# Semaphores set by SyncE ahead of a stage, one table load, and an in-place Newton step in a fused perceiver layer

## The reference

```python
B, S, dim, SKV, cdim, H, D = 16, 64, 256, 1601, 128, 16, 128
q = rmsnorm(layernorm(x) @ Wq, gq)               # per head, over D
k = rmsnorm(ctx @ Wk, gk);  v = ctx @ Wv         # per head
x = x + softmax(q @ k.T / sqrt(D)) @ v @ Wo
q, k, v = layernorm(x) @ W_qkv, each quantised by its own largest magnitude
x = x + softmax(q8 @ k8.T * scales / sqrt(hd)) @ v8 * v_scale @ W_out + b_out
x = x + causal attention with one key head and value head a token, chosen by argmax(softmax(x @ W_gate.T))
```

## Time and profile before

| what | us |
|---|---|
| median of 3 runs (lowest to highest) | 1481.54 (1479.16 to 1481.94) |
| the profiled execution's own time | 1480.01 |
| its span | 1478.0 |
| TensorE busy in it | 1386.3 (94%) |
| TensorE's weight loads | 936.6 (63%) |
| VectorE busy | 1259.4 (85%) |
| ScalarE busy | 1202.5 (81%) |
| GpSimd busy | 982.6 (66%) |
| query stage | 0 to 139.5 |
| key loop | 142.5 to 1237 |
| end of the loop | 1237 to 1318 |
| last stage | 1318 to 1478 |

### The profile page before, as it was taken

The page is one execution under the profiler, slowest core; times in us unless marked ns, Lnnn a source line. Parts: engine busy times, 40 slices in busy tenths (PEclk is TensorE's granted clock), DMA queues, the critical chain, the costliest instruction groups (busy, mean ns, idle before and its releaser), DMA issues. The chain is left out here.

```text
span 1478.0 us, 31543 instructions
## 1 busy us (share of the span) xinstructions
PE 1386.3 (94%) x5980; PEld 936.6 (63%) x5980; DVE 1259.4 (85%) x5006; ACT 1202.5 (81%) x4843; POOL 982.6 (66%) x1505
## 2 busy tenths in 40 slices
PE   5997999999999999999999999999999999966886
PEld 4664666666666666666666666666666666854554
DVE  6776888998989898889989898998998998756985
ACT  5886889898898989898988988898989887535763
POOL 4000788888989898889889898988888885010000
PEclk9998999999999999999999999999999999986998
DMA  4000000000000000000000000000000001000000
GB/s 143 38 1 1 1 2 24 4 21 16 10 23 1 24 1 23 2 23 2 23 13 13 23 1 25 1 23 2 23 1 27 22 30 64 1 1 1 8 7 16
DMA packets 9849, 25.30 MB, mean 17 GB/s; under 512 B 736, under 2 KB 6016, under 8 KB 9520
## 3 DMA queue, kind: packets, MB, share of 16 engines
q1 hardware_dynamic: 9648, 23.49, 4.4%
HBM read 22.44 MB, written 1.05 MB: 16 GB/s over the span
## 5 line engine op out<-in xcount | busy, mean ns | idle before, releaser
L1014 ACT ACTIVATE c_unused<-c_prod 124x128 f32<-124x128 f32 x1664 | 493.1, 298 | 83.6 <-DVE c_prod L1238 77.5
L1554 POOL TENSOR_TENSOR c_acc<-c_acc,c_prob 123x1024 f32<-123x1024 f32 (+1 forms) x192 | 461.9, 2406 | 23.9 <-ACT c_prob L1021 23.2
L1249 DVE CUSTOM_DVE_ANT_0 c_multiplied<-psK,c_c 124x128 f32<-124x128 f32 x1664 | 381.5, 285 | 57.0 <-PE psK L809 57.0
L808 PE MATMUL psK<-wkh,c_cTh 128*124 128x512 f32 x832 | 413.5, 497 | 10.9 <-DVE c_cTl L1277 9.2
L828 PE MATMUL psO<-c_prob,raw 123*128 123x512 f32 (+1 forms) x832 | 392.1, 594 | 0.0
L1238 DVE TENSOR_TENSOR c_prod<-psK,c_c 124x512 f32<-124x512 f32 x416 | 286.0, 688 | 53.4 <-PE psK L809 40.1
L809 PE MATMUL psK<-wkl,c_cTh 128*124 128x512 f32 x832 | 329.6, 396 | 0.0
L1014 ACT ACTIVATION_READ_ACCUMULATOR c_unused<-c_prod 124x1 f32 x1664 | 311.3, 187 | 0.0
L1260 DVE TENSOR_TENSOR c_prob<-psS,c_ss 124x512 f32<-124x512 f32 x416 | 265.7, 680 | 0.5 <-POOL c_ss L1537 0.5
L1021 ACT ACTIVATE c_prob<-c_prob,shift 124x1024 f32<-124x1024 f32 x208 | 236.6, 1137 | 0.4 <-DVE c_prob L1260 0.4
L808 PEld LDWEIGHTS psK<-wkh,c_cTh 128*124 128x124 f32 x832 | 154.2, 185 | 114.7 <-DVE c_ss L1249 47.5
(11 more groups left out here) (314 smaller groups left out, 2165.2 us busy)
## 6 DMA issues: line engine op xcount, KB each, us to landing
raw<-in_ctx SPq DMA_DIRECT2D x16, 799.5 KB
raw<-in_L_xattn_Wq SPq DMA_DIRECT2D x3, 512.0 KB, 9.5
xs<-in_x SPq DMA_DIRECT2D x1, 1024.0 KB, 5.8
big<-in_L_xattn_Wk SPq DMA_DIRECT2D x1, 1024.0 KB, 8.7
c_prod<-in_L_xattn_Wo SPq DMA_DIRECT2D x1, 1024.0 KB, 5.3
out<-s_y SPq DMA_DIRECT2D x8, 128.0 KB, 1.7
big<-in_L_ffn_W_qkv SPq DMA_DIRECT2D x1, 768.0 KB, 12.5
raw<-in_L_xattn_Wv SPq DMA_DIRECT2D x1, 768.0 KB, 4.1
```

What stands on the lines that cost most here:

```text
L808: nc.tensor.matmul(psK[0:ROWS, c % 2, :], cTh[:, slot, :], T.wkh[:, cols], start=True, stop=False)
L1014: last = nc.scalar.activation(unused[:, j, :], prod[:, k % 2, c // 2, j * CD:(j + 1) * CD], ACT.Copy, accum_out=ss[:, k % 2, 0, h:h + 1])
L1249: last = nc.vector.tensor_tensor_reduce(multiplied[:, j, :], psK[0:ROWS, 1, cols], c2[:, k % NT, :], 1.0, 0.0, ALU.mult, ALU.add, ss[:, k ...
L1554: nc.gpsimd.tensor_tensor(acc[0:rows, batch % 2, :], acc[0:rows, batch % 2, :], prob[0:rows, probs(s), :], ALU.add).then_inc(S.acc, 1)
```

## The change

1. `primed` is split into `signals` (makes the semaphores) and `set_signals` (sets them). The semaphores of the second and third stage are made ahead; SyncE sets those of the second while the first stage runs, behind its loads, and those of the third (68 of them) at the head of its block in the second. No block for either. Only the first stage keeps `primed`.
2. The table of functions is loaded in the first stage only.
3. Query stage: x comes in four DMAs and Wq in halves; statistics and normalisation go by halves of x; the sum of squares becomes two fp32r matmuls with GpSimd making the high part (an addition of a broadcast 0 that rounds to fp32r) and the low part; it moves one item later, beside the logarithm, and waits for `root` of two items before; the logarithm stands first on ScalarE. `scaled` goes and its value is written over the sum in PSUM. All of Wk's transposes and splits, and the splits of Wq's second to fourth quads, move into the first steps; GpSimd makes the low parts of Wq in pieces of 256 columns at the first twelve items, and clears `raw` in four pieces at items 20 to 23. The gain's maximum moves from items 28 and 30 to 25 and 28.
4. Key loop: `newton_start` writes its result over the bank, `newton_end` reads it there, and TensorE's wait at line 837 (and in `turn`) is for `dfull` instead of `dneg`.
5. `end`: `matrices(1)` and `segment(0)` before the denominators, `segment(1)` before `turn(2)`, with the other engines' order to match.
6. Last stage: five semaphores become two, `found` and `swept`.

```diff
@@ -133,10 +133,23 @@
+def signals(nc, ctx, plain, *loops):
+
+    zero, made = semaphores(nc, ctx, *plain), [semaphores(nc, ctx, *group) for group in loops]
+    return (zero, *made), [(sem, 0) for sem in zero] + [(sem, CREDIT) for group in made for sem in group]
+
+
+def set_signals(eng, sems):
+
+    for sem, value in sems:
+        eng.sem_clear(sem)
+        if value:
+            eng.sem_inc(sem, value)
...
@@ queries, SyncE
             sp.dma_start(wqkv, dram["L0_ffn_W_qkv"].rearrange("(k p) n -> p k n", p=P)).then_inc(S.wqkv, 16)
             sp.dma_start(wgate, dram["L0_ffn_W_gate"]).then_inc(S.wgate, 16)
-            sp.wait_ge(S.zeroed, 1)
+            set_signals(sp, T.later)
+            sp.wait_ge(S.zeroed, len(ZERO))
...
@@ queries, GpSimd, step(n, m, o)
+                pool.wait_ge(S.square, m + 1)
+                if m >= 2:
+                    pool.wait_ge(S.total, m - 1)
+                nc.gpsimd.tensor_tensor(squareh[:, m % 2, :], square[:, m % 2, :], blank[:, :].broadcast_to([P, BANK]), ALU.add).then_inc(S.squareh, 1)
+                pool.wait_ge(S.squareh, m + 1)
+                nc.gpsimd.tensor_tensor(squarel[:, m % 2, :], square[:, m % 2, :], squareh[:, m % 2, :].bitcast(F32), ALU.subtract).then_inc(S.squarel, 1)
...
@@ queries, TensorE
-                if m is not None:
-                    pe.wait_ge(S.square, m + 1)
-                    if m >= 2:
-                        pe.wait_ge(S.newton, m - 1)
-                    nc.tensor.matmul(psS[:, m % 2, :], T.ones[:, :], square[:, m % 2, :], start=True, stop=True).then_inc(S.total, 1)
...
+                    pe.wait_ge(S.squarel, o + 1)
+                    if o >= 2:
+                        pe.wait_ge(S.root, o - 1)
+                    nc.tensor.matmul(psS[:, o % 2, :], onesr[:, :], squareh[:, o % 2, :], start=True, stop=False)
+                    nc.tensor.matmul(psS[:, o % 2, :], onesr[:, :], squarel[:, o % 2, :], start=False, stop=True).then_inc(S.total, 1)
...
@@ cross_attention, TensorE, denominators
                 if den_bank(i, batch, half) is psM_all:
-                    pe.wait_ge(S.dneg, batch_done(i, batch, 2, half))
+                    pe.wait_ge(S.dfull, batch_done(i, batch, 2, half))
@@ cross_attention, TensorE, end
             def end(i, batch):
-                denominators(i, batch, 0)
-                pe.wait_ge(W.vTl, 2)
-                denominators(i, batch, 1)
                 matrices(1)
                 segment(0)
+                denominators(i, batch, 0)
+                denominators(i, batch, 1)
+                segment(1)
                 turn(2)
                 turn(3)
-                segment(1)
@@ cross_attention and self_attentions, ScalarE
-            nc.scalar.preload_act_table_set(LN_EXP)
@@ cross_attention, VectorE
             def newton_start(i, batch, half):
                 dve.wait_ge(S.dinv, batch_done(i, batch, 2, half + 1))
-                nc.vector.scalar_tensor_tensor(den[:, 2, :], den_bank(i, batch, half), -1.0, den[:, 1, :], ALU.mult, ALU.mult).then_inc(S.dneg, 1)
+                nc.vector.scalar_tensor_tensor(den_bank(i, batch, half), den_bank(i, batch, half), -1.0, den[:, 1, :], ALU.mult, ALU.mult).then_inc(S.dneg, 1)
             def newton_end(i, batch, half):
                 dve.wait_ge(S.dneg, batch_done(i, batch, 2, half + 1))
                 dve.wait_ge(S.norm, batch_done(i, batch, 2, half))
-                nc.vector.scalar_tensor_tensor(den[:, 3, :], den[:, 2, :], 2.0, den[:, 1, :], ALU.add, ALU.mult).then_inc(S.dfull, 1)
+                nc.vector.scalar_tensor_tensor(den[:, 3, :], den_bank(i, batch, half), 2.0, den[:, 1, :], ALU.add, ALU.mult).then_inc(S.dfull, 1)
```

More of the change, by code:

```diff
@@ L181, in load_context @@
     sp.dma_start(raw[FULL:ROWS, b, 0:REST, :], one[:, FULL * NT:SKV, :]).then_inc(sems[1], 16)
-PREP_SEMS = ("x gains wk wq0 wq1 wq2 wq3 consts gprod made stats moments centred lnT lnTh lnTl wkT wkTh wkTl wqh wql "
-             "gram gramh graml zeroed context m8 m2 sel causal iota selb wgate wqkv turn turned gT gtop gall")
+PREP_SEMS = ("x0 x1 x2 x3 gains wk wq0 wq1 wq2 wq3 consts gprod made stats moments centred lnT lnTh lnTl wkT wkTh wkTl wqh wql "
+             "wql0 onesr blank gram gramh graml zeroed context m8 m2 sel causal iota selb wgate wqkv turn turned gT gtop gall")
 Q_SLOTS = 3
 X_SLOTS = 2 * BANK // DIM
-ITEM_SEMS = "q square qgh qgl total log y half newton root qw out"
+ITEM_SEMS = "q square squareh squarel qgh qgl total log y half newton root qw out"
 def queries(nc, T, psum, dram):
@@ L252, in queries, with low_part @@
         gain_row, gain_all = psM[0:1, 0:P], psM[:, P:P + 1]
-        GAIN_AT, GAIN_ALL_AT = 28, 30
+        GAIN_AT, GAIN_ALL_AT = 25, 28
+        WK_AT, WQ_AT = ((0, 1), (2, 3)), (0, 1, 3)
+        wk_banks = (psO[:, 0, :], psO[:, 1, :], psT[:, :], psM[:, :])
+        FIRST = (NPAIR // 2) // PW
+        def low_part(m):
+            q, k, part = 1 + m // 4, m // 2 % WC, m % 2
+            return (q, k, part) if q < KC else None
+        ZERO_AT = (20, 21, 22, 23)
+        ZERO = [slice(2 * NT * CD * n // 4, 2 * NT * CD * (n + 1) // 4) for n in range(4)]
         def out(n):
@@ L337, in _ @@
                     last.then_inc(S.lnT, 1)
[L338 to L341, removed]
             def gram(q):
+                pe.wait_ge(S.wkTl, KC)
                 if q >= 2:
@@ L451, in _ @@
             act.wait_ge(S.consts, 5)
-            act.wait_ge(S.made, 1)
+            act.wait_ge(S.made, 2)
+            nc.scalar.activation(onesr[:, :], T.ones[:, :], ACT.Copy).then_inc(S.onesr, 1)
             def step(n, m, o):
+                if o is not None:
+                    act.wait_ge(S.total, o + 1)
+                    nc.scalar.activation(log[:, :], psS[:, o % 2, :], ACT.Ln, scale=1.0 / D, bias=T.eps[:, :]).then_inc(S.log, 1)
                 if n is not None:
@@ L515, in _, with statistics @@
-            for q in range(2):
-                wk_low(q)
-            for j in range(NPAIR // PW):
+            dve.wait_ge(S.consts, 2)
+            nc.vector.tensor_copy(T.identb[:, :], T.ident[:, :]).then_inc(S.made, 1)
+            def statistics(half):
+                for i in range(half * NPAIR // 2, (half + 1) * NPAIR // 2):
+                    if i % PW == 0:
+                        dve.wait_ge(x_there[i // PW], 16)
+                    nc.vector.bn_stats(stats[:, i, :], T.xs[:, i, :]).then_inc(S.stats, 1)
@@ L883, in turn @@
                 if q >= 2:
-                    pe.wait_ge(S.dneg, batch_done(LAST, 1, 2))
+                    pe.wait_ge(S.dfull, batch_done(LAST, 1, 2))
                 if q == 3:
@@ L1380, in end @@
             def end(i, batch):
-                weighed_low(0)
-                newton_start(i, batch, 0)
-                weighed_low(1)
-                newton_end(i, batch, 0)
-                weighed_low(2)
-                newton_start(i, batch, 1)
-                weighed_low(3)
-                newton_end(i, batch, 1)
+                for n in range(HB):
+                    weighed_low(n)
                 product_low(1)
                 next_segment(0)
+                for half in range(2):
+                    newton_start(i, batch, half)
+                    newton_end(i, batch, half)
                 wo_low(2)
+                next_segment(1)
                 v_low(2)
-                next_segment(1)
                 wo_low(3)
```

229 lines of the change are left out of this document (135 added, 94 removed).

## The result

The changed kernel takes **1523.22 us** (median of four runs, 1521.92 to 1523.56) beside 1481.74 us for the kernel before on the same chip: a ratio of 1.0282, 95% interval 1.0264 to 1.0300. The forecast was 1513 us, in a range of 1488 to 1542, with slower by over 0.2% at 0.85. The range holds the time; the middle was 10 us too low.

A forecast was written before the change was run, and what follows sets the result against it. TensorE was taken to bound the key loop, being busy 1004.24 of 1011.30 us. Against the profiled 1480.0 us, -15.5 + 1.1 + 36.6 + 17 - 4 - 2.5 = +32.7 gave 1512.7, rounded to 1513; range 1488 to 1542.

The forecast's parts named there:

- Step 1: Query stage: fp32r sums and moved work end it at 124 us instead of 139.5, -15.5 us.
- 3 for the gram and transposes between: Query stage: 3 us added between items 12 and 31, beside 18 x 2.75 = 49.5 us.
- the ring: Query stage: an item's sum waits for the root of two items before; closes at 2.66 us an item.
- Step 2: Start of the key loop: block and table load go, 68 semaphores ahead of `loaded` cost 5.1 us; +1.1 us.
- Step 3: Key loop: 15 TensorE waits of 2.44 us for `dfull`, +36.6 us; ten clock falls at 1.7, +17 us.
- rival B: Key loop: the clock falls after nearly every stall at the full 3.4 us; 1547 us, chance 0.10.
- an engine with slack: Key loop: `newton_end` falls from up to 1.29 to 0.69 us on VectorE, counted as 0.
- Rival A: Key loop: the stall comes but the clock stays up; 1496 us, chance 0.16.
- Rival C: Key loop: the wait at line 837 costs nothing; 1459 us, faster, chance 0.12.
- Step 4: End of the key loop: `matrices(1)` and `segment(0)` ahead of the denominators start the first segment earlier; -4 us.
- less work at half clock: End of the key loop: up to 2 us, taken with -2.9 us into the -4.
- Step 5: Last stage: without the block VectorE starts at 1318.3 instead of 1320.86, -2.5 us; its table load counts 0.

The follow-up runs named there:

- experiment 9: Newton step as before, `loaded` ahead of the 68 semaphores, old `end`, and the sum of squares as one fp32 matmul without GpSimd's two operations: 1471.12 us.
- experiment 4: The changed kernel with the four increments of `loaded` ahead of the 68 semaphores on SyncE: 1517.49 us.
- experiment 5: The changed kernel with `loaded` ahead of the 68 semaphores and `newton_end` ahead of the four sums of products in VectorE's tile: 1487.55 us.
- experiments 7 and 10: The same kernel twice: the changed kernel with the Newton step as before and `loaded` ahead of the 68 semaphores, new `end` kept: 1465.60 and 1464.02 us.
- experiment 1: The changed kernel with the Newton step as before (not in place, TensorE waits for `dneg`): 1468.32 us.
- experiment 3: The kernel before with only the in-place Newton step and its wait for `dfull`: 1535.65 us.
- experiment 2: The changed kernel, Newton step in place, with `newton_end` a tile earlier, right behind `newton_start`: 1484.91 us.
- experiments 7 to 11: Newton step as before, `loaded` ahead: new `end` 1465.60, 1464.02 us; old `end` 1461.83, 1461.32 us; old `end` with fp32 sum of squares 1471.12 us.
- experiments 10 and 11: Second pair with Newton step as before and `loaded` ahead of the 68 semaphores: new `end` 1464.02 us, old `end` 1461.32 us.
- the eleventh kernel: The changed kernel with the Newton step as before, `loaded` ahead of the 68 semaphores and the old `end`, second run: 1461.32 us.

## Why the prediction was right, and where it was off

**Step 1, query stage (-15.5, measured -13.3).** Parts of it hold. The first query matmul starts at 18.47, forecast 19.1. The sum of squares in fp32r is worth 6.1 to 6.5 us of stage (experiment 9). GpSimd's prices were 0.95 and 1.28 in the forecast and are 1.04 and 1.30. Item 12 begins on TensorE at 57.86 (forecast near 59) and the stage's end lies 12.3 us behind the start of item 31 (12.4); what is lost lies between, 57.86 to 113.83, 56.0 us instead of 52.5. Two terms of that sum were wrong. From item 12 to item 31 are 19 distances and not 18, which makes 2.75 us. And "3 for the gram and transposes between" is 5.4: the one item there that carries a gram stands 4.15 us behind the last (from square to square), 1.5 more than a quiet one, and others take 2.8 to 3.2. The choice of 2.75 for a quiet item was too high against 2.66, which gave 1.7 back. The 2.66 itself was forecast, but as the ring's figure, with VectorE as the fullest engine; ScalarE, priced at 2.64, is the one without idle time (experiment 9). Whether the ring would have held it at the same pace no run shows.

**Step 2, start of the loop (+1.1, measured +1.1).** Right to a tenth, and its mechanism is shown by experiment 4: the semaphores cost 4.97 us, and without them the removal of the block and of the table load would have been worth 3.9 us (4.30 to 0.42) where it cost 1.1.

**Step 3, key loop (+53.6, measured +55.2).** The waits are the ones forecast, 15 of 2.35 us (forecast 2.44). "Whatever holds TensorE there comes back almost whole" holds: 22.7 us of waits made the loop of experiment 5 about 21 us longer than that of experiments 7 and 10 (1101.1 against 1080.1 and 1080.4), 0.92 us for one. So 35.3 us of waits cost between 32.5 and 35.3, not 36.6. Against experiment 1, which lacks nothing but this edit, the loop of the changed kernel is 53.7 us longer (1131.0 against 1077.3). The waits taken off, 18 to 21 us are left for 12 falls of the clock, 1.5 to 1.8 each, where the forecast had 10 at 1.7, 17 in all. So the waits were sized a little too high and the falls a little too low, and that the sum fits as well as it does is in part luck. The 55.2 of the table holds 1.1 us that are not the edit's: in the kernel before the first transpose of the context stands 1.1 us ahead of the first split (142.68 and 143.79), in the changed one beside it. Experiments 1 and 3 show the whole, 5 parts the two.

Two readings of this step were wrong. It took the fall at the end of the loop to follow a pause of 2.50 us "shortly followed by one of 0.59"; but the second pause ends at 1241.05, so it began at 1240.46, when the clock had already fallen (1240.45). It had no part in the fall, and its absence in the loop was no argument against rival B. And the faster `newton_end` was put at nothing because VectorE is "an engine with slack". The duration came as forecast, 0.69 us at most, and nothing was gained; but experiment 2 shows that the reason doesn't carry: an average slack of 10% over the loop is not slack in the tile.

Rival A (the clock stays up) is out: 12, 13 and 15 falls in three kernels. Rival B had nearly all of them fall at 3.4 us each; in experiment 3 all did, and a fall costs about half of that, as forecast: it lasts 3.41 us, and dense work in it comes 1.7 us late. Rival C is out. The Trainium skill's rule, cited in the prediction, that only longer pauses bring the clock down ("TensorE: Matmul & The Clock Gate", "Why this matters for your kernels") differs from the measurement, and the measurement decides: pauses of 2.35 us brought it down 40 times out of 45.

**Step 4, end of the loop (-4, measured -1.7, and by experiments 7 to 11 no gain at all).** This step failed. I priced the move by when the first segment starts. That start did come earlier, 22.1 us behind the last transpose instead of 24.5 in the pair of experiments 10 and 11, but TensorE's work in the stretch is the same and its waits are 0.8 us longer in all, so the stretch ends 1.0 us later. The -1.7 of the table is the other term, "less work at half clock": the kernel before has a fall of 6.83 us there, the changed one none. Whether a fall comes doesn't hang on the order alone, since one came with the new order too.

**Step 5, last stage (-2.5, measured -2.5 for its start).** Right for the start and for the table load. Not foreseen: the rest of the stage takes 3.3 us longer, and its clock falls once more than before, at 1495.54. The few semaphores that changed in it are not the cause, since the eleventh kernel has them too and takes 157.5. Over the thirteen kernels this stage takes 157.2 to 157.8 us where the clock doesn't fall between the low stretches at its start and its end (three kernels), and 159.3 to 162.2 where it does (ten). The forecast had allowed for it only in its bounds.

The profiled execution is 9.2 us over the sum of 1512.7, which was made against the profiled one before: 2.2 in step 1, 1.6 in step 3, 2.3 in step 4 and 3.3 in the last stage, 9.4 by the rounded table.

## What to carry to other kernels

A buffer saved by working in place makes the next writer wait for the last reader and not for the first: look where in the order the last reader stands against that writer before doing it, for on a full engine each repetition costs nearly the whole distance. Setting semaphores in the shadow of another stage is good, but not in front of a signal that the next stage is waiting for; the order of the queue decides, 68 of them cost 5 us. The engine that sets a pace is found in one quiet repetition, by who has no idle time in it, not by the busy shares of a stage. And where TensorE is full, a pause costs more than its length, since the work behind it may run at half clock.

## What the runs showed of the hardware that was not expected

The length of a pause does not decide alone whether the clock falls. Fifteen pauses of 2.35 us a run, with dense work around, came with 12, 13 and 15 falls to 1.2 GHz in three kernels; fifteen of 1.51 us at the same place came with none. At the end of the loop a pause of 2.5 us brought a fall in four of the five kernels with the old order, and one of 1.97 us ahead of `matrices(1)` in two of the eight with the new.

Each of the 40 falls in the loop lasted 3.41 us and began 1.93 to 3.76 us after its pause had begun. Where two followed in neighbouring batches they were 71.68 us apart each time, in three kernels whose loops begin at different times, though an undisturbed batch takes 67.3 to 68.7 us and the pauses themselves stand 70.9 to 72.9 us apart. Counted from the neighbouring fall in steps of 71.68 us, the five pauses that brought none would have had theirs 1.70 to 1.90 us after their start (four of them) or 4.04 (one), outside the bounds of the others. So the 45 fit the reading that the place of a pause in time decides beside its length. This is read from the traces alone; no run shifted a pause to test it.

The last stage took between 157.2 and 162.2 us, by its falls of the clock; two orders of the same work can't be told apart by less than that from single profiles.
